# A two-layer graph network on one Trainium2 core: first edge pass over ranges of 32 nodes in four lanes, edge records in SBUF, blocks of 128 nodes

## The reference, cut to what matters

```
h = node_features @ node_fc_W + node_fc_b
hs, hd = (h[src], h[dst])
a = jnp.sum(hs * hd, axis=-1)
g = sigmoid(...three small networks over the edge's 64 features...)   # [E, 3]
alpha = _seg_softmax(a, dst, n)      # softmax over the edges of one destination
beta = _seg_softmax(g, dst, n)
h_att = segment_sum(alpha[:, None] * (hs @ sum_k node_att_W[k]), dst) / kk
h_rel = segment_sum(einsum('em,emf->ef', beta, hs @ rel_att_W[m]), dst) / mm
h_red = relu(concat([h_att, h_rel]) @ out_fc_W + out_fc_b)
```

## Time and profile before

| | us |
|---|---|
| median of three runs | 3838.8 |
| the profiled execution, its own time | 3869.9 |
| span of that execution, first to last instruction | 3868.0 |
| stage 1, to the first instruction of the pass | 684 |
| stage 2, first edge pass | 684 to 2224.5 |
| stage 3 | 2224.5 to 2384 |
| stage 4, second edge pass | 2384 to 3790 |
| stage 5 | 3790 to 3868 |

### The profile page before, as it was taken

One profiled execution on the slowest core, in us unless ns is written; L12 is line 12 of the kernel. 1 busy time (PEld: TensorE's weight loads), 2 busy tenths in 40 slices (PEclk: granted clock), 3 DMA queues, 4 the chain that ended last, 5 costly groups with the idle time before them and its releaser, 6 DMA issues. The chain is left out here.

```text
span 3868.0 us, 66746 instructions
## 1 busy us (share of the span) xinstructions
PE 2980.1 (77%) x17025; PEld 2039.3 (53%) x17025; DVE 2193.4 (57%) x5947; ACT 1479.6 (38%) x3759; POOL 1902.0 (49%) x1791
## 2 busy tenths in 40 slices
PE   5999999698989889898889936665665666656663
PEld 3444333466666666666666634554554555545552
DVE  8455210566666656666656673655555555555554
ACT  3777776233333334333333322222222222222221
POOL 0000000566666656666656502666666666666660
PEclk9999999799999989999999965776667777677675
DMA  2111121212212112222212102222222222222220
GB/s 69 57 45 45 55 76 39 60 48 52 52 49 50 50 47 52 49 52 51 49 48 50 39 2 60 72 70 70 70 71 72 70 70 71 71 71 72 71 69 19
DMA packets 231858, 217.93 MB, mean 56 GB/s; under 512 B 161623, under 2 KB 190124, under 8 KB 231787
## 3 DMA queue, kind: packets, MB, share of 16 engines
q0 software_dynamic: 70400, 144.29, 14.0%
q1 hardware_dynamic: 161387, 72.74, 7.5%
HBM read 203.65 MB, written 13.22 MB: 56 GB/s over the span
## 5 line engine op out<-in xcount | busy, mean ns | idle before, releaser
L984 POOL DMA_INDIRECT arena<-h_table,rec x880 | 976.4, 1110 | 545.8 <-issue 249.9
L1482 POOL DMA_INDIRECT arena<-kv_table,rec_sb x880 | 911.8, 1036 | 471.7 <-issue 235.3
L1030 PE MATMUL bank<-arena 128*128 128x375 f32 x1760 | 611.3, 490 | 0.0
L1528 PE MATMUL bank<-arena,probT 128*125 128x193 f32 x1760 | 513.8, 456 | 122.3 <-DVE probT L1646 65.6
L1528 PEld LDWEIGHTS bank<-arena,probT 128*125 128x125 f32 x1760 | 422.8, 265 | 179.7 <-DVE probT L1646 103.3
L1030 PEld LDWEIGHTS bank<-arena 128*128 128x128 f32 x1760 | 349.4, 199 | 302.0 <-issue 122.6
L1522 PE MATMUL bank<-top_run,ones 1*128 1x1 f32 x440 | 108.6, 313 | 367.8 <-DVE top_run L1625 196.4
L1111 DVE TENSOR_TENSOR arena<-onehot,rec 128x1500 f32<-128x1500 bf16 x220 | 376.5, 1711 | 0.0
L536 PE MATMUL bank<-eaT,wc 64*128 64x500 f32 x1200 | 360.8, 616 | 0.0
L1572 ACT COPY hotT<-bank 125x512 bf16<-125x512 bf16 x220 | 128.1, 582 | 580.4 <-remote 514.3
L1126 DVE CUSTOM_DVE_ANT_0 score<-bank,mask,m_old 125x512 f32<-125x512 f32 x220 | 165.2, 751 | 296.3 <-remote 178.8
(11 more groups left out here) (291 smaller groups left out, 4881.7 us busy)
## 6 DMA issues: line engine op xcount, KB each, us to landing
ea<-in_edge_attr SPq DMA_DIRECT2D x100, 250.0 KB
arena<-h_table,rec POOLq DMA_INDIRECT x880
arena<-kv_table,rec_sb POOLq DMA_INDIRECT x880
hbT<-hT_table SPq DMA_DIRECT2D x220, 62.5 KB
qb<-q_table SPq DMA_DIRECT2D x220, 46.9 KB
rec<-rec SPq DMA_DIRECT2D x220, 20.0 KB
rec<-rel_st SPq DMA_DIRECT2D x5, 781.2 KB
rec_sb<-rec SPq DMA_DIRECT2D x220, 4.0 KB
```

The costliest lines, as they stand in the source:

```text
L984: pool.indirect_dma_start(out=hs[:, k % RING, j, 0:D], out_offset=None, in_=h_table, in_offset=bass.IndirectOffsetOnAxis(ap=rec_v[:, k, j, ...
L1030: pe.matmul(bank[6 + k % 2][:, 0:M * BN], hs[:, k % RING, j, 0:D], hot_w_v[:, k % 2, j, :], start=(j == 0), stop=(j == GT - 1))
L1482: pool.indirect_dma_start(out=row_v[:, k % RING, j, 0:KV], out_offset=None, in_=kv_table, in_offset=bass.IndirectOffsetOnAxis(ap=rec_v[:, ...
L1528: last = pe.matmul(bank[4 + k % 2][0:BN, 0:KV + 1], probT_v[:, k % 2, j, :], row_v[:, k % RING, j, AD:RK], start=(j == 0), stop=(j == GT - 1))
```

## The change: windows of 32 nodes, four lanes, records that stay in SBUF

Blocks have 128 nodes (25 blocks, 3200 places, the last with 53 nodes), and node tensors have 128 partitions. The first edge pass works over windows of 32 nodes: 98 windows, 196 + 98 - 1 = 293 steps, rounded up to 296 (`STEPS0`). The four rows that a partition holds of a group (j = 0 to 3) are four lanes. Each lane has its own 32 output partitions, its own running maximum and its own attention sums; stage 3 merges the four.

POOL gathers each group once (196 x 4 gathers in place of 220 x 4) into one of four slots, and may overwrite a slot when the last step of the group before in it has copied it. ACT copies the rows from the slot to the step's own buffer (`copies`, new). The record table `rec0` is not written in the usual case: sources, destinations and weights lie in SBUF (`src_g`, `dst_g`, `w_g`), loaded at the start straight from the inputs in the order of the groups. The one-hot matrix is no longer turned for a mask; it is multiplied into the score's PSUM bank instead. Sums of `relations` are 96 x 129 (three weights by 32 nodes, with the weights' own sum in column 128).

```diff
@@ stage 1, SP @@
+                        def load_group(table, name):
+                            sp.dma_start(table[:, 0:COLS - GT].rearrange("p (g j) -> p g j", j=GT),
+                                         i[name][0:FULL].rearrange("(g p j) -> p g j", p=128, j=GT)).then_inc(groups_in, 16)
+                            sp.dma_start(table[0:TAIL, COLS - GT:],
+                                         i[name][FULL:].rearrange("(p j) -> p j", j=GT)).then_inc(groups_in, 16)
+                        for o in range(U):
+                            load_edges(o)
+                        load_group(dst_g, "dst")
+                        load_group(src_g, "src")
+                        for b in range(NB):
+                            sp.wait_ge(hT_sb, b + 1)
+                            sp.dma_start(h_table[b * BN:(b + 1) * BN, :], h_sb[:, b, :]).then_inc(h_out, 16)
+                            sp.dma_start(hT_table[:, b * BN:(b + 1) * BN], hT[:, b, :]).then_inc(h_out, 16)
@@ stage 1, ACT, ahead of the edge features @@
+                    act.wait_ge(h_out, 32 * NB)
@@ stage 1, DVE @@
+                    v.wait_ge(groups_in, 64)
+                    for b in range(1, WINS + 1):
+                        v.tensor_scalar((sel, sel2)[b % 2][:, 0:COLS], dst_g[:, :], float(WN * b), None, ALU.is_lt, ALU.add,
+                                        accum_out=below[:, b:b + 1]).then_inc(counted, 1)
@@ stage 2, POOL @@
+                    for g in range(GROUPS):
+                        k = g % RING0
+                        if g >= RING0:
+                            last_step = pool.value_load(reach_row[0:1, g - RING0:g - RING0 + 1], min_val=0, max_val=STEPS0 - 1)
+                            pool.wait_ge(copied, last_step + 1)
+                        gather(g, k)
+                        if g:
+                            pool.wait_ge(landed[(g - 1) % RING0], 64 * ((g - 1) // RING0 + 1))
+                            pool.sem_inc(ready, 1)
+                        if g == RING0 - 1:
+                            pool.memset(area_b, 0.0).then_inc(cleared_b, 1)
@@ stage 2, PE @@
-                        pe.matmul(bank[2][0:BN, :], hbT[:, k, :], hsT[:, k % 2, :], start=True, stop=True).then_inc(score_ps, 1)
+                        pe.matmul(bank[1 + k % 2][:, 0:128], far_rows[0:1, 0, :], far_rows[0:1, 1, :], start=True, stop=False)
+                        for j in range(GT):
+                            pe.matmul(bank[1 + k % 2][j * WN:(j + 1) * WN, 0:128], onehot_v[:, k % SH, j, :], big_ident[:, :],
+                                      start=False, stop=False)
+                        for j in range(GT):
+                            last = pe.matmul(bank[1 + k % 2][j * WN:(j + 1) * WN, 0:128], hbT[:, k % SH, :], hsT[:, k % 2, j * 128:(j + 1) * 128],
+                                             start=False, stop=True)
@@ stage 2, ACT @@
+                        g = act.value_load(row0(0, n), min_val=0, max_val=GROUPS - 1)
+                        slot = act.value_load(row0(2, n), min_val=0, max_val=RING0 - 1)
+                        act.wait_ge(ready, g + 1)
+                        act.wait_ge(cleared_a, 1)
+                        act.wait_ge(stepped, n + SU0 - SH + 1)
+                        act.copy(hs[:, k % SH, :, 0:D],
+                                 landed_rows[:, bass.ds(slot * GT * D, GT * D)].rearrange("p (j d) -> p j d", j=GT)).then_inc(copied, 1)
@@ stage 3, PE, per block @@
+                        for k in range(PER):
+                            pe.matmul(o[:, k * WN:(k + 1) * WN], att_acc[:, b * PER + k, 0:D], lane_sel[:, 0, :], start=True, stop=True)
+                        for k in range(PER):
+                            last = pe.transpose(o[:, BN + k * M * WN:BN + (k + 1) * M * WN], rel_acc[0:M * WN, b * PER + k, 0:D],
+                                                identf[0:M * WN, 0:M * WN])
```

More of the change, by code:

```diff
@@ L325, in build @@
             turned_from.append(side)
-            STORE_AT = {78 + 4 * n: n for n in range(TILES - 1)}
+            TOTS_AT, REACH_AT = 14, 76
             with nc.Block() as block:
@@ L351, in _ @@
                         sp.dma_start(dst, src).then_inc(weights_in, 16)
-                    with nc.allow_non_contiguous_dma(reason="columns of the second layer"):
+                    sp.wait_ge(blank, 4)
+                    sp.dma_start(x_sb[0:LAST, NB - 1, :], i["x"][N - LAST:, :]).then_inc(weights_in, 16)
+                    with nc.allow_non_contiguous_dma(reason="columns of the second layer, edges by group"):
                         sp.dma_start(w2[:, :], i["L0_gnn_rel_att_W2"].rearrange("m f -> f m")).then_inc(weights_in, 16)
@@ new lines, in turned_h @@
+                    def turned_h(b):
+                        act.wait_ge(hT_ps, b + 1)
+                        act.copy(hT[:, b, :], bank[b % 2][:, 0:BN]).then_inc(hT_sb, 1)
+                    turned_x(0)
+                    turned_x(1)
+                    projected(0)
+                    for b in range(NB):
+                        if b + 2 < NB:
+                            turned_x(b + 2)
+                        if b + 1 < NB:
+                            projected(b + 1)
+                        turned_h(b)
@@ L1149, in body @@
                             take(s, k)
-                        if inside(edge, k, 4):
-                            hot(*step_of(s, k, 4))
-                        if inside(edge, k, 2):
-                            maximum(*step_of(s, k, 2))
-                            weigh(*step_of(s, k, 2))
-                    rounds(v, body, 4)
+                        if inside(edge, k, 3, SU0):
+                            hot(*step_of(s, k, 3, SU0))
+                        if inside(edge, k, 2, SU0):
+                            maximum(*step_of(s, k, 2, SU0))
@@ L1160, in build @@
+                        if inside(edge, k, 3, SU0):
+                            weigh(*step_of(s, k, 3, SU0))
+                    v.memset(area_a, 0.0).then_inc(cleared_a, 1)
+                    v.wait_ge(cleared_a, 2)
+                    v.wait_ge(cleared_b, 1)
+                    rounds(v, body, 3, STEPS0, SU0)
         with ExitStack() as c3:
@@ L1202, in build @@
             q_sb = sem3("q_sb3")
-            tables = [sem3(f"tables3_{k}") for k in range(W)]
+            tables = sem3("tables3")
             with nc.Block() as block:
@@ new lines, in outs @@
+                    def outs(b):
+                        pe.wait_ge(sum_sb, 2 * (b + 1))
+                        if b >= 8:
+                            pe.wait_ge(added, b // 4 - 1)
+                        o = bank[3 + b // 4 % 2][:, b % 4 * D:(b % 4 + 1) * D]
+                        for m in range(M + 1):
+                            last = pe.matmul(o, sumT[:, b % 3, m, :], w_fold[:, m, :], start=(m == 0), stop=(m == M))
+                        last.then_inc(out_ps, 1)
+                    sums(0)
@@ L1278, in _ @@
+                        pe.matmul(q_ps[:, 0:AD], x1T[:, b % W, :], w_kvq[:, KV:], start=True, stop=True).then_inc(kvq_ps, 1)
+                    turn_x(0)
+                    turn_x(1)
+                    for b in range(NB):
+                        keys(b)
+                        if b + 2 < NB:
+                            turn_x(b + 2)
                 @block.scalar
@@ new lines, in _ @@
+                    for n in range(quads):
+                        add_bias(n)
+                        if n + 2 < PIECES:
+                            rescale(n + 2)
+                    for j in range(PER):
+                        lanes = slice(j * WN, (j + 1) * WN)
+                        step(v.tensor_copy(has[lanes, :], some[lanes, j::PER]))
+                        step(v.tensor_copy(hasnt[lanes, :], none[lanes, j::PER]))
+                    v.wait_ge(added, quads)
+                    v.wait_ge(gates_e, 1)
@@ L1370, in _ @@
+                    step(v.tensor_tensor(y, y, h_all, ALU.add))
                     step(v.tensor_tensor(y, y, x_all, ALU.subtract))
```

1188 lines of the change are left out of this document (571 added, 617 removed).

## The result

The changed kernel takes 4294.75 us (median of 4 runs, 4292.22 to 4301.96), the kernel before 3842.74 us beside it: 1.118 times as long, 95% interval 1.116 to 1.120. The forecast was 3580. The profiled executions (spans 3868.0 and 4290.9 us) divide at the first and the last maximum of the edge passes. These are the rows for that line of the kernel before and of the changed kernel: durations in ns (min/median/max), then the start of the first and of the last.

The account below looks back on a forecast made before the run. TensorE was taken to bound the first edge pass (6.17 of 6.93 us a step). 3868 + 48 + 4 - 10 - 324 + 25 + 6 - 8 = 3609 us span, 3611 with 1.9 around it, at 0.992 3580 us; range 3430 to 3760.

Parts of the forecast that it names:

- 37 + 295 x 4.0 = 1217 us: First edge pass: 37 us until its first attention sum, then 295 steps of 4.0 us; 324 us less.
- VectorE's term: First edge pass: VectorE's operations 2.05 us a step, with four register loads 3.2 us, under ScalarE's.
- forecast 3.1 us: First edge pass: TensorE's work per step, summed over its products and turns; bounds 2.7 and 4.7.
- forecast 3.75: First edge pass: ScalarE's us per step, 2.5 of operations plus register loads and waits; bounds 2.7 and 4.3.
- forecast 1090 us: First edge pass: POOL's 784 gathers, register loads and clearing, or 3.7 us per step; bounds 975 and 1250.
- Rival E: First edge pass: TensorE stays at the lower clock level, steps of 5.6 us, kernel 4050 us; chance 0.08.
- Stage 1's start: Edge-feature loop starts at 148 us, not 100, after node tables land behind two small-run loads: +48, bounds -25 and +204.
- Rival C: Start of stage 1: the small runs load at 195 a us, start 156 us later, kernel 3735 us; chance 0.15.
- The counts: Stage 1: VectorE's 98 counts at 0.89 us end at 211 us, hidden because TensorE asks for them at 228.
- The forecast's 37 us: Start of the first edge pass: POOL gathers four groups (20 us), then clears 11 us, and VectorE waits: 37 us.
- Stage 3: Stage 3 some 75 us for 36 at a middle clock, +40; with the last part's 15 less, +25, bounds 0 and +60.
- Second pass and final store: Second edge pass slightly larger operations and weights, +6 us, bounds -20 and +30; final store of 128 partitions faster, -8 us.

Follow-up runs that it names:

- e5: The changed kernel as it is, measured again in a set where the kernel before took 3393.0 us: 3465.8 us, 1.022 of the kernel before.
- e16: Changed kernel with TensorE, ScalarE and VectorE working in a new order, some register loads moved ahead of waits: 3392.4 us, 1.001 of the kernel before.
- e7: Changed kernel without the first edge pass's gathers after the first four groups (stale rows): 3462.5 us, kernel before 3393.0 us.
- e17: The kernel of e16 without the first edge pass's gathers after the first four groups (stale rows): 3391.0 us, kernel before 3386.4 us.
- e6: The kernel before as it is, profiled again in the set of e5: 3384.8 us.
- e19: The kernel of e17, with ScalarE and VectorE loading four steps' numbers at once: 3779.7 us, kernel before 3890.1 us.

## Why the prediction was wrong, step by step

**The step that failed** is "37 + 295 x 4.0 = 1217 us". It failed twice, and unequally: 2.05 us of the 2.39 us a step are delayed signals, which the sum put at nothing; 0.34 us are VectorE's term, 3.2 us in the sum and 4.3 measured.

- *The delays.* The prediction took the pass before, 6.93 us a step, as TensorE's 6.17 us of work and some waits, and the forecast step as sums of work. The trace of before already had 263 us of delays in this pass. Rows 2 showed them: `remote 100.3` on POOL's line, 79.5 on ScalarE's, 18.6 on VectorE's, in a program of one core. They were passed over. That a step which TensorE fills for 5.7 us hides most of a burst of four gathers (5.0 us), and a step of 4.3 us with bursts of eight (10 us) does not, fits these numbers; no run varies the one without the other. The forecast noted that a slot comes free when ScalarE has copied it, but not that this can bunch the gathers of two groups.
- *TensorE*: forecast 3.1 us. Without delays it is 934.15 us over 289 steps, 3.23. The eight instructions of L1038 took 0.43 us, and 0.66 us at the lower clock level, against the 0.45 that was taken. Right. The rule of the Trainium skill (TensorEngine Tiling (Array Packing), Key Properties), by which each change of the tiling mode drains the engine and which would have made it 3.5, is not needed to explain 3.23.
- *ScalarE*: forecast 3.75. Busy 2.30 plus 1.37 idle before L1067, where two of the three loads stand, is 3.67. Right; waits on top of it (0.41 for VectorE's maximum, 0.2 before two small copies) make 4.3.
- *VectorE*: forecast 3.2, and this is the term that was mis-sized. Busy 2.00 us was right (2.05). Each load was counted at 0.29 us, its TENSOR_LOAD alone. In e5 VectorE stands idle before each of the four operations that follow a load:

```profile
L1133 DVE TENSOR_TENSOR hot_w<-onehot,w_g 128x384 f32<-128x384 bf16 x294 | 165.5, 563 | 157.1 <-issue 133.0 <-PE bank L1038 24.0
L1145 DVE TENSOR_SCALAR_CACHE_REDUCE junk<-bank,m_st 128x128 f32<-128x128 f32 x293 | 102.8, 351 | 220.1 <-issue 212.1 <-PE bank L1015 8.0
L1156 DVE SCALAR_TENSOR_TENSOR att_acc<-att_acc,shrink,bank 128x129 f32 x293 | 102.3, 349 | 155.0 <-issue 143.8 <-PE bank L1038 11.2
L1120 DVE TENSOR_SCALAR gone<-dst_g,base 128x4 f32 x293 | 72.0, 246 | 144.2 <-PE bank L1015 103.4 <-issue 40.8
```

That is 0.53, 0.75, 0.53 and 0.49 us, 2.30 a step, and with 2.00 busy it is 4.30 of the 4.34 us. These stretches hardly vary (the maximum's lies between 0.70 and 0.84 us in nine steps of ten), so little of them is waiting for another engine. Without delays VectorE with its loads, and not ScalarE, sets the step; e16, whose VectorE loads three numbers in place of four, took 4.08 us.
- *POOL*: forecast 1090 us. A gather took 0.95 us on average, now that VectorE's 1500 columns are gone; the rule of the Trainium skill (SBUF — State Buffer, SBUF: two separate sides) agrees with that too. And e7 and e17 show that POOL is not on the path without delays (1274.7 and 1204.2 us, against 1279.2 and 1204.7 with gathers).
- *Rival E* put the crossing at 4.9 us a step and was right in that: the pass passed it, but by another mechanism. TensorE's clock was 0.73 with TensorE busy for 57%; where signals were on time it was 0.86 with 75% (e5) and 1.00 with 100% (e6). The low clock goes with the waits, and even at 0.73 TensorE's work is 3.6 us a step (1066.56 / 294.5); the other 2.8 us are waits.
- *Stage 1's start* (+48, bounds down to -25) was too late: the loop over edge features starts at 79.7 us, 20 us sooner than before, and not at 148. SP's queue in the changed kernel:

```profile
25.28 15.75 SPq L379 DMA_DIRECT2D dst_g<-in_dst  x1
...
41.50 14.34 SPq L379 DMA_DIRECT2D src_g<-in_src  x1
55.89 0.49 SPq L388 DMA_DIRECT2D h_table<-h_sb  x1
```

24960 runs of 16 bytes went in 15.75 us, 1585 a us, nearly three times the fastest row that the prediction had (557). Rival C is out. The counts ran from 93.8 to 181.0 us, 970 ns each; with the loop this early they were not hidden, and TensorE waited 10.8 us for them at L599. The first gather started at 672.3 us against 689.0. VectorE had cleared its area by 685.2 us, but POOL clears its own behind the first 16 gathers, to 703.1 us, and VectorE waits for that. It took back the 17 us and 3 more, and this stage came out at +3. The forecast's 37 us ahead of its steps had this wait in them.
- *Stage 3* (+25, measured +56 in both kinds of set). The sums were 75 us in the forecast and took 96:

```profile
L1258 PE MATMUL bank<-lane_sel,att_acc x200: 261/401/422, 2610.1 to 2705.9; 128*128 128x32 f32 x100
```

TensorE was busy 91 of 103 us there at a clock of 0.52, nearly all of it at the lower of its two levels; the forecast had taken a middle clock.
- *Second pass and final store*: -3 and -7 against +6 and -8. Right.

Without delays the parts of e6 and e5 differ by +1, +30, +56, +1.5 and -7.5, from 3382.7 to 3464.1 us: slower than before too, by 2.2% in the timed runs. There the gain in the first pass is not there to be had, because the kernel before's step is 5.70 us and 220 x 5.70 is nearly 296 x 4.34.

## What to carry to other kernels

Read who ended a wait before trusting a busy share: on one core a wait that `remote` ended is a signal that came late, and no engine's work fills it. How much of it is lost shows only beside a trace without delays: in the changed kernel 604 us before the maximum carry the label and the idle time there grew by 541; with bursts of four 298 us carry it and it did not grow. When a kernel issues gathers from POOL, ask how many will follow each other without a pause, and whether one step of the other engines covers them; where two slots of a ring come free together, a burst is twice as long. More and shorter steps pay every fixed cost again: here the register loads cost ScalarE 1.37 and VectorE up to 2.3 us of a step of 4.34. Time the kernel before beside every experiment: here it moved by 12% from one set to the next.

## What the runs showed of the hardware that was not expected

- The same program takes about 3385 to 3395 or 3840 to 3890 us from one set of runs to another (the kernel before; where a set has 7 to 13 runs they lie within 0.9%). One chip was of one kind in one set and of the other in a later one, so it is not simply the chip. What brings it about stays open; shown is only that stretches without gathers do not have it.
- In a set with delays TensorE's finished work is seen 6 to 8 us late while POOL issues gathers 1.25 us apart, but not at once: in the first 2 us of a burst signals pass in 0.04 to 0.24 us, and later ones get stuck until about its end (VectorE's late maxima start within some 2 us of the end of the burst's last gather, on either side). Bursts of four with pauses of 2.0 us or more (3.1 in the median) nearly avoid the loss (55 us against 602). Why a gap of 0.30 us between gathers does not let a signal through stays open, and a shorter pause was not tried.
- On ScalarE a load of four registers takes 910 ns where one takes 281, and 147 ns for each number come on top (medians of e19 and e5).
